# Two rows per statistics operation, and a re-ordered step, in a two-layer graph kernel on one core

## What is computed

```python
h = relu(layernorm(x))
triple = concat([h[src], h[dst], relation_embedding[edge_type]], axis=1)
c = triple @ W1 + b1
b = leaky_relu(c @ w2, 0.01)
alpha = softmax of b over the edges of each target
x = x + leaky_relu(segment_sum(c * alpha, dst), 0.01)
h = relu(layernorm(x))
agg = segment_sum(h[src], dst)
x = x + where(a node has edges, agg, h)
```

## Time and profile before

| | us |
|---|---|
| median of three executions | 1811.62 (1809.88 to 1812.3) |
| the profiled execution | 1812.44 |
| its span, first to last instruction | 1807.6 |
| PE busy | 1489.1 (82%) |
| VectorE busy | 1538.6 (85%) |
| ACT busy | 1373.4 (76%) |
| GpSimd busy | 1231.9 (68%) |

### The profile page before, as it was taken

How to read it: one execution, slowest core, us unless ns; L and a number is a source line. 1 busy time by engine, 2 the same in 40 slices (tenths; PEclk the granted TensorE clock), 3 DMA queues, 4 the chain that set the end, 5 groups by cost and what they waited for, 6 DMA issues and landing times.

```text
span 1807.6 us, 37626 instructions
## 1 busy us (share of the span) xinstructions
PE 1489.1 (82%) x12132; PEld 1349.5 (75%) x12132; DVE 1538.6 (85%) x5561; ACT 1373.4 (76%) x3555; POOL 1231.9 (68%) x1069
## 2 busy tenths in 40 slices
PE   1489999999999999999999962677767767776767
PEld 0489999999999999999999952555555555555556
DVE  5768999999999999999999686788878888788886
ACT  0578888888888888888888723677777777787777
POOL 4778877677767776777774007777777777777772
PEclk9999999999999999999999986799999999899998
DMA  6455666566666666665665563566766766666543
GB/s 147 123 137 153 171 169 167 170 168 166 169 169 169 167 169 170 169 168 169 169 171 138 154 196 88 143 193 179 195 177 194 197 178 186 184 190 185 160 109 117
DMA packets 465338, 297.91 MB, mean 165 GB/s; under 512 B 32123, under 2 KB 434357, under 8 KB 465142
## 3 DMA queue, kind: packets, MB, share of 16 engines
q1 hardware_dynamic: 430390, 243.09, 48.4%
q0 software_dynamic: 34752, 52.43, 11.5%
HBM read 208.14 MB, written 104.34 MB: 173 GB/s over the span
## 4 chain that ended last, share of the span: by engine, by line
PE 52%; ACT 11%; DVE 10%; POOL 9%; DMA 9%; issue 7%; POOLq 0%; SPq 0%; DVEq 0%; ACTq 0%
POOL xe L962 9%; DMA xe<-x_d,idx_t 8%; PE c_p L1316 7%; ACT cs L1242 6%; PE c_p L1317 6%; PE t_p L1304 6%; PE c_p L1321 5%; PE c_p L1319 5%; ACT cs L1245 4%; PE y_p L1342 4%; PE t_p L1303 3%; PE t_p L1306 3%; PE t_p L1305 3%; PE y_p L1344 3%; PE y_p L1345 3%
## 5 line engine op out<-in xcount | busy, mean ns | idle before, releaser
L962 POOL DMA_INDIRECT xe<-in_x,idx_t x522 | 680.9, 1304 | 255.2 <-issue 153.3
L962 POOL DMA_INDIRECT xe<-x_d,idx_t x522 | 531.7, 1019 | 268.8 <-issue 137.1
L1011 DVE BATCH_NORM_STATS2 st<-xn 128x6 f32<-128x128 f32 x1566 | 349.7, 277 | 157.5 <-DMA xe<-x_d,idx_t 132.2
L1242 ACT ACTIVATE cs<-xn,nbias,rstd 128x128 f32<-128x128 f32 x783 | 326.2, 479 | 54.4 <-DVE nbias L1055 54.4
L1242 ACT ACTIVATE an<-xn,nbias,rstd 128x128 f32<-128x128 f32 x783 | 326.9, 483 | 16.5 <-DVE nbias L1055 16.5
L1013 DVE BATCH_NORM_STATS2 st<-xe 128x6 f32<-128x128 f32 x1044 | 243.4, 274 | 0.0
L1268 ACT ACTIVATE lr<-y_p 128x390 f32<-128x390 f32 x261 | 129.6, 497 | 137.3 <-PE y_p L1345 131.8
L1245 ACT ACTIVATE ae<-xe,nbias,rstd 128x128 f32<-128x128 f32 x522 | 226.2, 482 | 0.0
L1245 ACT ACTIVATE cs<-xe,nbias,rstd 128x128 f32<-128x128 f32 x522 | 225.2, 478 | 0.0
L1316 PE MATMUL c_p<-w1a,th 128*128 128x129 f32 x1044 | 216.1, 289 | 0.0
L1317 PE MATMUL c_p<-w1b,th 128*128 128x129 f32 x1044 | 202.6, 276 | 0.0
(11 more groups left out here) (176 smaller groups left out, 3478.8 us busy)
## 6 DMA issues: line engine op xcount, KB each, us to landing
xn<-in_x SPq DMA_DIRECT2D x130, 384.0 KB, 6.5
x_d<-xn SPq DMA_DIRECT2D x130, 384.0 KB, 7.5
xn<-x_d SPq DMA_DIRECT2D x130, 384.0 KB, 4.2
out<-xn SPq DMA_DIRECT2D x130, 384.0 KB, 3.8
plr<-place_d SPq DMA_DIRECT2D x65, 256.0 KB, 3.6
tyr<-types_d SPq DMA_DIRECT2D x65, 256.0 KB, 5.6
xe<-in_x,idx_t POOLq DMA_INDIRECT x522, 3.8
xe<-x_d,idx_t POOLq DMA_INDIRECT x522, 3.5
```

What stands on the lines that cost most here:

```text
L962: nc.gpsimd.indirect_dma_start(out=xe_of(L, u)[:, e, :], out_offset=None, in_=a, in_offset=bass.IndirectOffsetOnAxis(ap=idx_t[:, j:j + 1], ...
L1011: v.bn_stats(st[:, j % 2, UN * at + i, :], xs_of(L, u)[:, i, :])
L1242: a(own[:, i, :], xs_of(L, u)[:, i, :], ACT.Relu, bias=nbias[:, j % 2, c:c + 1], scale=rstd[:, j % 2, c:c + 1])
```

## The change

It has these parts.

1. One `bn_stats` takes two rows: its input is written as `p d r`, so the elements of the two rows alternate, the even half is one row and the odd half is the other. For two units of three node rows the pairs are rows 0-1, then 2-3 and 4-5 in the second unit's turn; the two edge rows are a pair. Variance and mean then need no joining.
2. The variance (one operation in place of six) is made at the end of the step in which the batch's last statistics are made, and this step is `lo - ahead - 2`, one later than before. The factors are made in the next step, ahead of its statistics.
3. ACT makes a batch's roots ahead of the normalization in both layers; in the first layer its step begins with `messages` of unit s-1 and ends with `slopes` of unit s-23.
4. PE's step is turn, aggregate, messages.
5. The last batches have 4, 2, 2 and 1 units.
6. In the second layer VectorE adds a pair to `x` before the step's factors and statistics.
7. In the prologue VectorE counts the fetched rows before it waits for the weights. Of `x` only super-block 0 is loaded early; 1 is loaded when the second set of windows is released, and 2 to 4 behind the first tables.

```diff
-        st = sb("st", [P, 2, LC, 6], f32)
+        st = sb("st", [P, 2, LC, 3], f32)
...
-                for q in range(XPRE):
-                    for rows_, g0, g1, np_ in parts_of(x, q):
-                        sp.dma_start(xn[0:np_, q, g0:g1, :], rows_).then_inc(x_in.of(q), 16)
-
+                first_x(0)
+                sp.wait_ge(k_win[1], TC)
+                first_x(1)
                 sp.wait_ge(k_places, UE)
...
-                dve.wait_ge(k_in, 16 * NIN)
-                dve.wait_ge(k_relT, 1)
-                v.tensor_copy(relT[:, 0:P + RB], t_p[:, 0, 0:P + RB]).then_inc(k_relTs, 1)
-
                 for k in range(TC):
                     dve.wait_ge(k_rowl[k], 16)
...
                     v.tensor_copy(win_at[0][:, k:k + 1], s0c[:, k:k + 1]).then_inc(k_win[0], 1)
 
+                dve.wait_ge(k_in, 16 * NIN)
+                dve.wait_ge(k_relT, 1)
+                v.tensor_copy(relT[:, 0:P + RB], t_p[:, 0, 0:P + RB]).then_inc(k_relTs, 1)
...
-            LNB, SMB = cut((2, 2, 4, 4), LB), cut((), SB_)
+            LNB, SMB = cut((2, 2, 4, 4) + 30 * (LB,) + (4, 2, 2, 1), LB), cut((), SB_)
...
-                    end = lo - ahead - 3
+                    end = lo - ahead - 2
...
                 for q in range(2):
                     load_tables(q)
+                for q in range(2, XPRE):
+                    load_x(L1, x, q)
...
-                        for i in range(UN):
-                            v.bn_stats(st[:, j % 2, UN * at + i, :], xs_of(L, u)[:, i, :])
-                        for e in range(UE):
-                            last = v.bn_stats(st[:, j % 2, LB * UN + UE * at + e, :], xe_of(L, u)[:, e, :])
+                        if at % 2 == 0:
+                            two_rows(j, UN * at, xn[:, n % XS, u % QU * UN:u % QU * UN + 2, :])
+                        else:
+                            two_rows(j, UN * at - 1, xn[:, n % XS, u % QU * UN - 1:u % QU * UN + 1, :])
+                            two_rows(j, UN * at + 1, xn[:, n % XS, u % QU * UN + 1:u % QU * UN + 3, :])
...
+                        last = two_rows(j, LB * UN + UE * at, xe_of(L, u))
...
+                def two_rows(j, c, rows_):
+                    return v.bn_stats(st[:, j % 2, c:c + 2, :].rearrange("p c t -> p (c t)"), rows_.rearrange("p r d -> p d r"))
+
+                def variances(L, s):
+                    j = L.batch_end.get(s)
...
+                    ln.settle()
+                    wait(dve, L.rstd, j)
+                    v.tensor_scalar(var[:, :], st[:, j % 2, :, 2], 1.0 / D, EPS, ALU.mult, ALU.add).then_inc(L.var, 1)
...
-                    j = L.batch_end.get(s - 1 if piece < 3 else s - 2)
+                    j = L.batch_end.get(s - 1)
...
+                    if piece == 4:
+                        ln.settle()
+                        v.scalar_tensor_tensor(nbias[:, j % 2, :], st[:, j % 2, :, 1], -1.0, r, ALU.mult, ALU.mult).then_inc(L.rstd, 1)
...
+                    ln_piece(L1, s, 0)
                     for piece in range(6):
                         softmax_piece(s, piece)
+                    ln_piece(L1, s, 1)
                     if v_ % 2 == 1:
                         slope1(v_ // 2)
                     ln_piece(L1, s, 2)
-                    ln_piece(L1, s, 5)
+                    ln_piece(L1, s, 4)
                     stats(L1, s)
-                    ln_piece(L1, s, 6)
                     if v_ % 2 == 1:
                         add1(v_ // 2)
+                    variances(L1, s)
...
                 for s in range(L1.first_step, NU + LAG + 2):
-                    slopes(s - LAG - 1)
+                    messages(s - 1)
+                    if s - 1 in L1.batch_end:
+                        roots(L1, L1.batch_end[s - 1])
                     norm(L1, s + L1.ahead)
                     turned(s + 1)
-                    messages(s)
-                    if s - 1 in L1.batch_end:
-                        roots(L1, L1.batch_end[s - 1])
+                    slopes(s - LAG)
...
                 for s in range(L2.first_step, NU):
-                    norm(L2, s + L2.ahead)
                     if s - 1 in L2.batch_end:
                         roots(L2, L2.batch_end[s - 1])
+                    norm(L2, s + L2.ahead)
...
                     turn(s + 1)
+                    aggregate(L1, s - LAG)
                     messages(s)
-                    aggregate(L1, s - LAG)
```

More of the change, by code:

```diff
@@ L633, in _, with first_x @@
             def _(sp):
+                def first_x(q):
+                    for rows_, g0, g1, np_ in parts_of(x, q):
+                        sp.dma_start(xn[0:np_, q, g0:g1, :], rows_).then_inc(x_in.of(q), 16)
                 for to, from_, landed in ((dsti, dst_e, k_dst), (srci, src_e, k_edge), (typi, typ_e, k_edge)):
@@ L1009, in stats, with ln_piece @@
                         at = u - LNB[j][0]
[L1010 to L1013 removed]
+                        if at % 2 == 0:
[3 more added lines that the diff above has]
+                            two_rows(j, UN * at + 1, xn[:, n % XS, u % QU * UN + 1:u % QU * UN + 3, :])
+                        if at % 2 == 0 and u == NU - 1:
+                            two_rows(j, UN * at + 2, xn[:, n % XS, u % QU * UN + 2:u % QU * UN + 4, :])
+                        last = two_rows(j, LB * UN + UE * at, xe_of(L, u))
                         if u == LNB[j][1] - 1:
                             ln.mark(last)
[L1017 to L1018 removed]
+                def two_rows(j, c, rows_):
+                    return v.bn_stats(st[:, j % 2, c:c + 2, :].rearrange("p c t -> p (c t)"), rows_.rearrange("p r d -> p d r"))
+                def variances(L, s):
+                    j = L.batch_end.get(s)
                     if j is None:
                         return
[L1021 to L1022 removed]
+                    ln.settle()
+                    wait(dve, L.rstd, j)
+                    v.tensor_scalar(var[:, :], st[:, j % 2, :, 2], 1.0 / D, EPS, ALU.mult, ALU.add).then_inc(L.var, 1)
+                def ln_piece(L, s, piece):
+                    j = L.batch_end.get(s - 1)
+                    if j is None:
+                        return
+                    t0, t1 = (tiny[:, c, :] for c in range(2))
                     r = rstd[:, j % 2, :]
@@ L1048, in ln_piece @@
                         ln.mark(v.scalar_tensor_tensor(r, t1, 1.5, rstd0[:, :], ALU.add, ALU.mult))
-                        if L is L2:
-                            ln.settle()
-                            k = UN * (hi - lo)
-                            ln.mark(v.tensor_tensor(r[:, 0:k], r[:, 0:k], none_t[:, UN * lo:UN * hi], ALU.mult))
-                    if piece == 6:
-                        ln.settle()
-                        v.scalar_tensor_tensor(nbias[:, j % 2, :], msum, -0.5, r, ALU.mult, ALU.mult).then_inc(L.rstd, 1)
+                    if piece == 3 and L is L2:
+                        ln.settle()
+                        k = UN * (hi - lo)
+                        ln.mark(v.tensor_tensor(r[:, 0:k], r[:, 0:k], none_t[:, UN * lo:UN * hi], ALU.mult))
+                    if piece == 4:
+                        ln.settle()
+                        v.scalar_tensor_tensor(nbias[:, j % 2, :], st[:, j % 2, :, 1], -1.0, r, ALU.mult, ALU.mult).then_inc(L.rstd, 1)
                 mF, mB, d, w, sF, sB = (soft[:, c, :] for c in range(6))
@@ L1380, in _ @@
                 def _(sp):
-                    for q in range(XPRE):
+                    for q in range(2):
                         sp.wait_ge(x_in.of(q), x_in.count(q))
```

39 lines of the change are left out of this document (9 added, 30 removed).

## The result

The changed kernel takes 1786.87 us (median of four runs, 1784.31 to 1787.17), the kernel before 1811.96 in the same comparison. The ratio is 0.9861, 95% interval 0.9848 to 0.9873: faster by 25.1 us. Forecast were 1800.2 and a range of 1790 to 1822. The sign was right; the size was more than twice what was forecast, and the time lies 3 us under the range. Ratios here compare executions in the faster of the two states that a kernel can show, while medians are over all executions.

The account below looks back on a forecast made before the run. PE was taken to bound the first layer and GpSimd's queue the second. Prologue 5.5, start 1.7 and last batches 4.2 gave 11.4 us off 1812.44, 1801.0, set to 1800.2 for the median; range 1790 to 1822.

Parts of the forecast that it names:

- What bounds the kernel: Steady steps: PE bounds the first layer, GpSimd's queue the second; lightening VectorE ends no steady step of either.
- PE's order: First layer's steps: reordering PE's full work costs nothing; zero, bounds 0 and +4 us in all.
- Layer 2's stream: Second layer's gathers: GpSimd does not wait for its ring, so 690 us stay.
- Two-row statistics: VectorE's statistics: 0.43 us per two-row operation, 1.08 per unit, 0.10 more than now; net nothing.
- Rivals one and two: First layer: VectorE becomes the bound, 1838 us, chance 0.16; or is just full, 1806 to 1816 us, chance 0.08.
- the fourth: Second layer: VectorE is the bound after all and the operation costs 0.325: 75 us less, 1737, chance 0.03.
- Prologue: Before the first layer: last window gather and first layer's first gather 5.5 us earlier, bounds 0 and 8.
- Start: First layer until PE is full: turn(12) 4.0 us earlier, low PE clock costs about 2.3; 1.7 kept, bounds -1 and 5.
- The third rival: Start: x loads and slow PE clock take back the prologue's gain; only last batches count, 1807.4 us, chance 0.08.
- Last batches: Second layer's end: batches of 4, 2, 2, 1 gain 4.2 us, bounds 1 and 8.

Follow-up runs that it names:

- a2_again: The changed kernel with PE's step put back to turn, messages, aggregate, on an undisturbed chip: 1799.63 us, ratio 0.9938 to the kernel before.
- a3_again: The kernel before with only the two-row statistics and the shorter variance work added, on an undisturbed chip: 1809.64 us, ratio 0.9977.
- b1_prologue_undone: The changed kernel with the prologue of the kernel before, relT copy first and all first x loads at once: 1793.34 us, ratio 0.9901.
- b3_fp32_first: The changed kernel with both edges' fp32 message products ahead of both edges' bf16 products, each edge's first product with start=True: 1777.37 us, ratio 0.9809.
- c2_fp32_first: The changed kernel with both edges' fp32 message products ahead of the bf16 ones, only the bank's first product clearing it: 1776.74 us, ratio 0.9805.

## Why the prediction was right or wrong

- **What bounds the kernel: half right.** PE in layer 1 and GpSimd's queue in layer 2 are the bounds, and VectorE's 7 us less of 200 in layer 1 gave nothing, as a2_again shows. The inference from it, that nothing in the steady stretches could move, was the error.
- **PE's order: this step failed.** "PE is full, and the order of full work costs nothing ... Zero, bounds 0 and +4 us." Being full said only that the order would count in full, with whatever it did to PE's own durations. It brought 10.4 us alone and cost 11.7 when undone. The rows to see it stood beside those that were used: the earlier trace rows has 0.44 for the aggregation's first product, and the next ones in the same timeline have 0.39. The bound excluded a gain without a reason.
- **Layer 2's stream: this step failed too.** "GpSimd does not wait for its ring, so 690 us stay." It did not wait, but its own instructions were 11 ns longer with VectorE's old work, and the stream measured 684.1 us. On undisturbed chips it is 684.1 to 686.7 us in the twelve profiled kernels with the new VectorE work (two of them with operations added), 685.6 in the mean, and 689.5 and 688.9 in the two with the old. So some 3.6 us (2.2 at the least) go with VectorE's work, the rest of the 5.4 is scatter of one profile, and a3_again has 686.1 with that work alone. Which operation it is stays open: putting back the small ones or doubling the selects did not show it.
- **Two-row statistics: mis-sized, the sum unharmed.** The forecast had 0.43 us per operation, a middle of 0.37 and 0.48. In the timeline above they start 0.33 apart (0.34 in the median), and a contiguous selection of 256 elements takes 0.325: the jump of 512 bytes costs next to nothing, as far as two different operations can be compared; contiguous statistics of 256 elements were not run. A unit's statistics are 2.5 x 0.33 = 0.83 us in place of 0.98, instead of 1.08. A faster VectorE gives little here, so the total did not suffer. Rivals one and two, which needed 0.52 and 0.48, had 0.24 together and are refuted, and so is the fourth, which had layer 2's stream 75 us shorter; the rule of the Trainium skill, page "SBUF — State Buffer" (the two sides of SBUF), that an access to another 16-byte line pays a penalty, is not borne out for this operation: with the same reserve, 0.02 us or less in 0.34 is left for it.
- **Prologue: the sum right, its parts not.** 5.46 us against 5.5, and 5.5 when undone. The first window gather went from 19.87 to 16.15, 3.7 us earlier where the sum had 1.7. The slowest window gather landed after 7.0 us instead of 9.8, 2.8 sooner where it had 4. The last one started at 27.79 instead of 34.95, 7.2 earlier where it had 5.5, and the chain to the first gather gave 1.7 of it back: VectorE now waits 2.62 us for the last landing, 0.51 before. That the errors cancel is luck.
- **Start: mechanism right, size off.** The wait for unit 21 went, the variance of batch 12 to 19 became late, PE stood and its clock fell, all as written. But 5.1 us of pause and the low clock took everything: turn(12) gained 0.3 us beyond the prologue, not 1.7. The third rival (the prologue's gain taken back as well) fell: b1_prologue_undone cost 6.5 us.
- **Last batches: right in kind, 3.1 for 4.2.** Of the tail's gain the batches hold 3.2 us. VectorE's new work alone shortens the tail by 1.6 (a3_again), so the parts overlap. The small operations count here too, which the sum had at nothing: five of them back cost 2.7 us in the tail, where a short batch's factors are waited for.
- **The range** joined bounds that for both failed steps excluded a gain. At its other end the bounds were added wrongly: 0, -1, -4 and 1 us make 4 us slower, 1816, and not the 1808 that the prediction gives for them. With the order's 12 us the same sum gives 1788, close to the time measured; that the missed 5.4 us of the stream and the overrated start and tail then cancel is luck.

## What to carry to other kernels

An engine at 200.00 of 200 us is not at its floor: count its pieces of work in the window and look for instructions of one form with two durations. On PE, put bf16 blocks ahead of transpositions, not of fp32 products, and do the fp32 products of a step together. Short first batches have to last: here two more of them moved the pause to the next long batch, and ten took it away. And split each run's time by stage before reading its total: the small operations' run had the expected total from a place that its theory did not name.

## What the runs showed of the hardware that was not expected

- An fp32 product of 128 to 130 columns behind bf16 products takes 0.27 us instead of 0.22; two transpositions there take 0.22. A transposition's weight load takes 141 ns, the product's 192. Behind four fp32 transpositions of 16 columns the two take 0.27.
- Statistics of 256 elements that jump by 512 bytes at each start 0.33 us apart, where a contiguous selection of 256 elements takes 0.325.
- Most of GpSimd's gathers take 1.00 us; one in six with the old VectorE work and one in nine with the new take longer, 1.12 and 1.10 us in the mean, without any wait in the trace. Over 522 of them this was some 3.6 us. What lengthens them is not shown.
- A product with start=True drops what a product with another region of the same bank had gathered before (b3_fp32_first); with start on the bank's first product alone both regions keep their sums (c2_fp32_first).
- On a chip where the engines wait for remote, PE's shorter step did not show in the total: ratio 0.9992 (0.9949 to 1.0035) there, 0.9944 (0.9928 to 0.9961) on an undisturbed one. The intervals touch, so that it is worth less there is not shown.
